# A convolution, spectral and feed-forward hybrid on one core: the first normalisation on GpSimd, a new order of work, two images per loop body

## The reference, cut to what matters

```python
# layer 0
h = depthwise_conv_7x7(x) + conv_b
h = (h - mean_c(h)) * rsqrt(var_c(h) + 1e-5) * ln_g + ln_b        # the "first normalisation"
h = gelu(h @ w1 + b1) @ w2 + b2
x = h * layer_scale + x
# layer 1, on tokens t = x as (image, 3136, 96)
u = relu(bn1(ln(t) @ aw1))                                        # second normalisation
X = fft over the 3136 tokens of u
y = ifft(relu(complex scale and shift of X)).real
t = t + bn2(y @ aw2)
t = t + quantised_linear2(relu(quantised_linear1(ln(t))))         # third normalisation
```

## Time and profile before

| | |
|---|---|
| runs shown | 4677.69 us median of 3 (4676.67 to 4680.09) |
| the profiled execution | 4678.17 us; its span 4676.4 us, so 1.8 us lie around the span |
| busy in the span | PE 3989.9 us (85%), DVE 3461.5 (74%), ACT 2285.2 (49%), POOL 1390.6 (30%) |
| chain that ended last | PE 36%, DVE 30%, time without a named wait ("issue") 12%, ACT 2%, POOL 2%, DMA 1% |
| first in the chain by line | PE 993 (M2) 9%, PE 987 (M1) 7%, PE 1026 (B) 5%, DVE 892 (B) 5%, DVE 831 writing `h_norm` 4%, DVE 831 writing `xn2` 4% |
| TensorE's clock, mean | 0.966 of full |
| DMA | 532.48 MB at a mean of 114 GB/s |

### The profile page before, as it was taken

The page is one execution under the profiler, slowest core; times in us unless marked ns, Lnnn a source line. Parts: engine busy times, 40 slices in busy tenths (PEclk is TensorE's granted clock), DMA queues, the critical chain, the costliest instruction groups (busy, mean ns, idle before and its releaser), DMA issues.

```text
span 4676.4 us, 88192 instructions
## 1 busy us (share of the span) xinstructions
PE 3989.9 (85%) x22802; PEld 2808.8 (60%) x22802; DVE 3461.5 (74%) x11833; ACT 2285.2 (49%) x4610; POOL 1390.6 (30%) x1572
## 2 busy tenths in 40 slices
PE   5999969888888888888888888888888888888885
PEld 3444436666666666666666666666666666666664
DVE  2333346788888888888888888888888888888876
ACT  2444424455555555555555555555555555555543
POOL 1111233333332333333333333333333232333331
PEclk8999979999999999999999999999999999999986
DMA  6666524344444444444443333343444444444331
GB/s 172 166 169 172 163 71 107 94 111 115 111 113 113 111 112 115 109 113 115 110 114 105 98 102 107 102 108 105 108 113 114 111 113 114 112 112 113 100 91 49
DMA packets 420416, 532.48 MB, mean 114 GB/s; under 512 B 220047, under 2 KB 378493, under 8 KB 404413
## 3 DMA queue, kind: packets, MB, share of 16 engines
q1 hardware_dynamic: 405920, 510.40, 40.6%
q10 hardware_dynamic: 14272, 20.04, 1.7%
HBM read 295.18 MB, written 235.12 MB: 113 GB/s over the span
## 4 chain that ended last, share of the span: by engine, by line
PE 36%; DVE 30%; issue 12%; ACT 2%; POOL 2%; DVEq 1%; DMA 1%; ACTq 0%; POOLq 0%; SPq 0%
PE psum L993 9%; PE psum L987 7%; PE psum L1026 5%; DVE minus L892 5%; DVE xn L831 4%; DVE h_norm L831 4%; DVE plus L892 4%; DVE stats L809 3%; PE psum L1035 2%; PE psum L1007 2%; DVE act L875 2%; PE psum L1015 2%; PE psum L1049 2%; DVE h L922 1%; PE psum L1062 1%
## 5 line engine op out<-in xcount | busy, mean ns | idle before, releaser
L683 POOL TENSOR_TENSOR scales<-sums,minus_half 112x4 f32<-112x4 f32 (+1 forms) x480 | 636.6, 1355 | 2191.8 <-DVE sums L824 2191.8
L712 POOL TENSOR_TENSOR both<-plus,minus 96x224 f32<-96x224 f32 (+1 forms) x1024 | 618.2, 623 | 587.3 <-DVE minus L892 502.9
L993 PE MATMUL psum<-hid,w_sb 128*96 128x448 f32 x1344 | 592.8, 580 | 6.5 <-ACT hid L748 2.0
L987 PE MATMUL psum<-hn,w_sb 96*128 96x448 f32 x1344 | 557.2, 547 | 8.4 <-ACT h L796 6.9
L767 ACT ACTIVATE uw<-psum,spec 96x224 f32<-96x224 f32 (+1 forms) x1024 | 445.6, 511 | 157.5 <-PE psum L1026 154.9
L386 PE MATMUL c_psum<-c_xt,c_toeplitz 128*112 128x448 f32 x1152 | 476.6, 551 | 50.3 <-ACT c_xt L328 26.9
L414 DVE TENSOR_SCALAR c_h<-c_psum,c_bias 112x448 f32<-112x448 f32 x192 | 199.0, 1036 | 413.1 <-PE c_psum L386 413.1
L892 DVE SCALAR_TENSOR_TENSOR plus<-psum,spec,uw 96x224 f32<-96x224 f32 (+1 forms) x1024 | 426.8, 417 | 63.5 <-ACT uw L767 63.0
L748 ACT ACTIVATE hid<-psum,b_sb 128x448 f32<-128x448 f32 x672 | 419.7, 635 | 104.1 <-PE psum L987 61.9
L892 DVE SCALAR_TENSOR_TENSOR minus<-psum,spec,uw 96x224 f32<-96x224 f32 (+1 forms) x1024 | 425.8, 416 | 0.0
L1035 PE MATMUL psum<-aw_sb,both 96*112 96x96 f32 x3712 | 410.3, 263 | 4.7 <-ACT hid L748 4.7
(11 more groups left out here) (85 smaller groups left out, 6549.5 us busy)
## 6 DMA issues: line engine op xcount, KB each, us to landing
outer_spectrum<-outer SPq DMA_DIRECT2D x448, 168.0 KB
inner<-outer_spectrum SPq DMA_DIRECT2D x32, 2016.0 KB
c_xpad<-x SPq DMA_DIRECT2D x96, 392.0 KB, 11.2
h_tokens<-c_h SPq DMA_DIRECT2D x24, 1568.0 KB, 8.4
h<-h_tokens SPq DMA_DIRECT2D x32, 1176.0 KB, 13.3
x_sb<-x SPq DMA_DIRECT2D x32, 1176.0 KB, 7.3
residual_stream<-t SPq DMA_DIRECT2D x224, 168.0 KB, 2.1
inner_inverse<-unmixed SPq DMA_DIRECT2D x224, 168.0 KB, 2.3
```

The costliest lines, as they stand in the source:

```text
L683: nc.gpsimd.tensor_tensor(scales[which][:, at:at + w], su[:, :, 5], minus_half[:, 0:w], ALU.pow).then_inc(ready.sem, 1)
L712: last = nc.gpsimd.tensor_tensor(both[:, c % 2, m, 0:w, k * PT // 2:(k + 1) * PT // 2], half(plus), half(minus), ALU.subtract if k else AL ...
L987: pe.matmul(bank("M1", c, m, CW, 128), w1_sb[:, m * 128:(m + 1) * 128], hn[:, c * CW:(c + 1) * CW], start=True, stop=True).then_inc(m1_mad ...
L993: last = pe.matmul(dst, w2_sb[:, m, :], hid[:, c % 2, m, :], start=(m == 0), stop=(m == KF - 1))
```

## The change

- L0N moves from DVE to POOL: DVE's branch and the helper `normalize` go, POOL gets the same four `tensor_scalar` per chunk, with `add` in place of `subtract`; for the first normalisation `sums[..., 3]` therefore holds minus the mean (factor -0.5).
- `variances` no longer writes `sums[..., 3]` for the second normalisation, where nothing reads it; in the other two that instruction goes ahead of the product.
- `STAGES` and `LATER` get new numbers for every step and engine.
- The first steady turn (n = 2) is written out, and the loop has 14 iterations of two turns.

```diff
 STAGES = {
-    1: {"M1": (-3, 11.8, NC), "M2": (7, 11.8, NC), "T": (13, 11.8, NC), "W1": (22, 11.8, NC), "A": (27, 11.8, NC)},
-    2: {"B": (11, 9.3, ND), "W": (24, 9.3, ND), "IB": (28, 8.8, ND)},
-    3: {"AP": (3, 11.5, NC), "S2": (8, 11.5, NC), "N2": (14, 11.5, NC), "T2": (18, 11.5, NC), "F1": (20.5, 12, NC),
-        "G": (25, 11.5, NC), "F2": (32, 11.5, NC)},
-    "next": {"L0S": (34, 3.4, NC), "L0N": (72, 3.3, NC), "HT": (79, 2.8, NC)},
-    "fetch": {"FETCH": (9, 11.5, NC - 3)},
-    "fetch next": {"FETCH NEXT": (78, 1, 3)},
+    1: {"M1": (-0.5, 11.7, NC), "M2": (6.0, 11.8, NC), "T": (12.5, 11.7, NC), "W1": (22.0, 11.9, NC),
+        "A": (25.5, 12.7, NC)},
+    2: {"B": (8.0, 8.7, ND), "W": (18.0, 9.9, ND), "IB": (27.5, 8.9, ND)},
+    3: {"AP": (2.0, 11.1, NC), "S2": (6.5, 11.0, NC), "N2": (12.5, 11.4, NC), "T2": (17.5, 10.8, NC),
+        "F1": (21.0, 12.0, NC), "G": (23.5, 11.8, NC), "F2": (31.0, 12.1, NC)},
+    "next": {"L0S": (35.5, 3.9, NC), "L0N": (94.5, 4.0, NC), "HT": (88.5, 3.0, NC)},
+    "fetch": {"FETCH": (28.5, 10.5, NC - 3)},
+    "fetch next": {"FETCH NEXT": (103.0, 1.4, 3)},
 }
 LATER = {
-    "act": {"W": -0.5, "G": -0.5},
-    "dve": {"B": 3, "M2": 2, "T": 2, "W1": 1, "F2": 2, "AP": 1, "S2": 1, "L0N": -1, "W": -2},
-    "pool": {"B": 4, "T": 3, "S2": 2, "F1": 1},
-    "sp": {"M2": 3},
+    "act": {"F2": 0.5, "T2": -1.0, "B": -0.5, "IB": -0.5, "HT": 0.5, "A": 0.5},
+    "dve": {"B": 1.0, "M2": 0.5, "T": 2.5, "F2": 9.0, "S2": 1.5, "L0N": 0.5, "G": -0.5, "N2": -0.5, "L0S": -10.0},
+    "pool": {"B": 6.5, "T": 5.0, "S2": 5.0, "L0N": -21.0, "L0S": -7.5},
+    "sp": {"M2": -2.0, "IB": -0.5, "A": 12.0, "FETCH": -8.0, "FETCH NEXT": 10.5},
     "pe": {},
 }
...
-            with eng.Fori(2, NB - 1) as n:
-                turn("steady", n)
+            turn("steady", 2)
+            with eng.Fori(0, (NB - 4) // 2) as pair:
+                turn("steady", pair * 2 + 3)
+                turn("steady", pair * 2 + 4)
...
+                    if name == "L0N":
+                        if c == 0:
+                            pool.wait_ge(ln0_ready.sem, ln0_ready.at(n + 1))
+                        b, j = before(n + 1, c, NC, 4)
+                        pool.wait_ge(ht_made.sem, ht_made.at(b, j))
+                        pool.sem_inc(passed, 1)
+                        for j in range(CH):
+                            q = CH * c + j
+                            last = nc.gpsimd.tensor_scalar(
+                                h_norm[:, c % 4, j, :].rearrange("p (k c) -> p k c", c=CC), h[:, :, q, :],
+                                sums[0][:, q, 3:4], scales[0][:, q:q + 1], ALU.add, ALU.mult)
+                        last.then_inc(h_normed.sem, 1)
...
+                if which != 1:
+                    nc.vector.tensor_scalar(su[:, :, 3], su[:, :, 0], 0.5 if which else -0.5, None, ALU.mult)
                 nc.vector.scalar_tensor_tensor(out=su[:, :, 4], in0=su[:, :, 2], scalar=C / 4.0, in1=su[:, :, 2],
-                                               op0=ALU.mult, op1=ALU.mult)
-                nc.vector.tensor_scalar(su[:, :, 3], su[:, :, 0], 0.5, None, ALU.mult).then_inc(step.sem, 1)
+                                               op0=ALU.mult, op1=ALU.mult).then_inc(step.sem, 1)
...
-                    if name == "L0N":
-                        if c == 0:
-                            dve.wait_ge(ln0_ready.sem, ln0_ready.at(n + 1))
-                        b, j = before(n + 1, c, NC, 4)
-                        dve.wait_ge(ht_made.sem, ht_made.at(b, j))
-                        normalize(0, 0, h_norm[:, c % 4, :, :].rearrange("p q (k c) -> p q k c", c=CC),
-                                  h[:, :, part, :].rearrange("p k q c -> p q k c"), CH * c).then_inc(h_normed.sem, 1)
```

More of the change, by code:

```diff
@@ L825, in variances @@
                                                op0=ALU.add, op1=ALU.add).then_inc(seen.sem, 1)
[L827 to L834, removed]
             def turn(kind, n):
@@ L916, in turn @@
                         dve.wait_ge(xt2_made.sem, xt2_made.at(*before(n, c, NC, 2)))
-                        normalize(2, c, xn2[:, c % 2, :, :], t2_rows[:, c % 2, :, :], 0).then_inc(xn2_done.sem, 1)
+                        for j in range(CH):
+                            at = CH * (c % 2) + j
+                            last = nc.vector.tensor_scalar(xn2[:, c % 2, j, :], t2_rows[:, c % 2, j, :], sums[2][:, j, 3:4],
+                                                           scales[2][:, at:at + 1], ALU.subtract, ALU.mult)
+                        last.then_inc(xn2_done.sem, 1)
                     if name == "G":
```

## The result

The changed kernel takes **4620.35 us** (median of 4 runs, 4611.43 to 4629.68), the kernel before, run beside it, 4678.77: a ratio of 0.9876, with a 95% interval of 0.9854 to 0.9897. It is faster by 1.2%. The prediction said 4400 us with a range of 4240 to 4570: right in the sign, wrong in the size, and outside the range. Its profiled execution took 4616.74 us, its span 4614.9.

A forecast was written before the change was run, and what follows sets the result against it. No engine alone bounds the kernel: TensorE and VectorE wait for each other in order. TensorE busy 105.4 plus waits 8.0 gives a turn of 113.4 us, 9.6 less, times 29 is 278: 4678 - 278 = 4400 us, range 4240 to 4570.

The forecast's parts named there:

- the jump: Loop jump over two turns: at most 2.41 us for each of 14 jumps, taken as 0.6, +8 us in all.
- (f): TensorE at B 1 waits for `inner`, whose DRAM round trip from A 6 has less cover: 3.5 us a turn, bounds 0 and 6.
- (a) to (c): TensorE's waits at T2 for N2 and at T for W1's bank go: some 4.2 of 4.27 us at T2 0, most of 3.2 at T.
- (e): TensorE at M1 0 waits for ScalarE's copy for HT 6, now that nothing stands between: 1.0 us a turn.
- (g): TensorE's W1 3 waits for its bank, emptied by VectorE's late M2 4: 2.0 us a turn, bounds 0 and 4.27.
- (h): TensorE's waits at A 6 and F2 6 at the turn's end keep their cause: 1.5 us a turn.
- The sum of waits: TensorE's waits left per steady turn in the new order: 8.0 us.
- (d): VectorE sheds 7.1 us (first normalisation) and 0.6 (unused mean) a turn, so the small waits for it go.
- the normalisation: First normalisation on GpSimd: 300 ns an instruction, 8.4 us a turn (7.5 to 18.7), cost 0 for the last three steps.
- held ports: GpSimd's new instructions slow VectorE beside them: left at 0 a turn, bounds 0 and 6.0 us.
- Slower: GpSimd paces the turn's end: Rival: slow GpSimd instructions delay HT 6; gain used up from 1.1 us each, 4817 us at 1.5; chance 0.12.
- Less: Rival: waits only move and ports are held, so only VectorE's work counts: 4.1 us a turn, 4560 us; chance 0.20.

The follow-up runs named there:

- e1: The changed kernel with one turn per loop body instead of two: 4494.95 us, ratio 0.9607 to the kernel before.
- e4: The kernel before with nothing changed but two turns per loop body: 4865.68 us, ratio 1.0396.
- e2: The changed kernel with SyncE's stores of A and the fetches of the next turn 6 places earlier: 4551.19 us, ratio 0.9722.
- e3: The changed kernel with both one turn per loop body and SyncE's earlier stores of A and next fetches: 4443.75 us, ratio 0.9496.
- e8: e3 with GpSimd's fifth step of the first normalisation ahead of its power for T 6: 4442.56 us, ratio 0.9495.
- e6: e3 with the first normalisation back on VectorE: 4442.42 us, ratio 0.9493 to the kernel before.
- e11: e3 with the unused mean of the second normalisation written again: 4442.74 us, ratio 0.9494.
- e14: e3 with GpSimd subtracting the mean instead of adding minus the mean: 4553.97 us, ratio 0.9732.
- e7: The kernel before, order kept, with only the first normalisation moved to GpSimd, subtracting the mean: 4970.42 us, ratio 1.0610.
- e9: e8 with B a place later on every engine: 4623.64 us, ratio 0.9871 to the kernel before.
- e12: e9 with SyncE's three fetches for the next turn ahead of A 5's store: 4508.25 us, ratio 0.9628.
- e13: e7 with GpSimd adding minus the mean instead of subtracting the mean: 4759.35 us, ratio 1.0177.

## Why the prediction was right or wrong

**The failed step is the jump.** "Bounds 0 and 2.41 per jump ... I take 0.6, +8 us in all": measured per iteration it was 9.0, 125 us (e1), and 13.3 in the old order (e4), both beyond the upper bound. The bound came from VectorE's idle at its own jump, another engine with another body; the row that only one queue fetched in the steady turns was read rightly as a warning, and then priced by a row that cannot show the new case. The Trainium skill's sentence gave the right event, and the prediction gave it a size from that same row. Nor did any term hold the clock: behind each of the 13 waits M1 0 takes 4.5 to 4.9 us for 2.52.

**The second failed step is a sentence of (f)**: "ScalarE's A 5 may wait for A 3's, and what it waits comes off (f), since the edge then begins later". A 5 does wait for A 3's store, and TensorE for A 5 3.4 us at HT 1, but nothing came off: B 1 still waited 57.4 / 16 = 3.6 us for `inner` in the turns that have no jump, which is (f)'s 3.5. The two add up because the wait stands ahead of A 6, and (f) is counted from A 6 on. The queue was named and its price left at nothing; e2 put it at 69 us, and with one turn per iteration (e1 to e3) it is 51.

These two are 176 us of the 220 (e3). **The third is the clock at M1 0.** In e3 TensorE's busy time is 1.9 us a turn over the 105.4 predicted, and M1 0 alone is 2.15 us longer than M1 1 at the edge shown. The sum took off what a slow M2 1 had cost at the old wait and put nothing in for the matmuls behind the new waits at HT.

**What held.** (a) to (c): T2's and T's waits went, 236.0 to 10.2 and 94.1 to none. (e): M1 0 waits 0.8 to 1.0 us for the last HT copy, as predicted. (f): 3.6 against 3.5 in the turns that have the wait (2.1 in e3), and `inner` proved to be the end that the turn hangs on (e8). (g): 42.3 us, 1.5 a turn against 2.0, but mostly at W1 1 and not at W1 3. (h): nothing was left of the 1.5; A 6 and F2 6 wait no more.

**What was right by luck.** The sum of waits: e3 has 7.7 us a turn where 8.0 stood, but 2.1 of them are at HT for GpSimd, which stood at 0, and (f) and (h) came out smaller by 2.9. Also (d) and the normalisation. VectorE's 7.1 us and the mean were counted as part of the gain; e6, e8 and e11 show that in the new order they are worth nothing in sum, and the gain is the order's alone. One instruction cost 0.41 us alone and 0.54 in the mean, not 0.30. In this profile's groups of GpSimd in the steady turns:

```profile
L703 POOL TENSOR_SCALAR h_norm<-h,sums,scales 112x96 f32<-112x96 f32 x812 | 425.6, 536 | 104.5 <-PE psum L984 104.4
```

That is 15 us a turn against 8.4, and "Cost 0" for the last three steps became 0.9 a turn at HT, 2.1 in e3.

The Trainium skill, "SBUF — State Buffer", "Who interferes with whom", has GpSimd and a two-port VectorE instruction exclude each other. The trace agrees: a step of four took 1.62 us at 2767.7, with VectorE idle, and 3.45 at 2772.1, beside F2's and G's instructions. The prediction left held ports at 0 for VectorE's side: N2's instruction took 453 ns in the mean where it took 353, but also 408 in e6, so only a part of that is the normalisation's, and TensorE's waits for N2 are 10.2 us in all.

**The rivals.** "Slower: GpSimd paces the turn's end" did not happen, but it was near: it is what e14 does to e3, at 0.84 us an instruction in the mean, and what e7 does to the kernel before. The sign of the mean, which is part of the change and which the prediction did not price, is what kept it away. "Less" gave 4560 for the reverse of the truth: it had VectorE's work count and the order not. The range ended at 4570, just above this rival; with a jump bounded at 2.41 us, 34 us in all, nothing in the sum asked for more.

**A version that beats both** is e3, 4443.75 us, 5.0% under the kernel before; e6, with no normalisation on GpSimd at all, is as fast.

## What to carry to other kernels

Price a longer loop body by the instructions of its largest engine and not by the turn that it saves: here a doubled body cost TensorE a fetch and a slow spell at every jump, 125 of the 185 us that the rest of the change gave (e1). When a step is moved in an in-order DMA queue, ask of each transfer behind it who waits for it and what it waits for: A 3's store cost 69 us here (e2), and fetching `t_old` sooner gave back 115 of the 181 us that e9 had lost (e12). After a gain, look for the end that the period hangs on (here A 6 to B 1): work taken off another engine was then worth nothing (e8, e11). And give the clock a term: waits of 3.2 us in all ahead of M1 0 took another 2 us with them (e3).

## What the runs showed of the hardware

- A GpSimd `tensor_scalar` of 112x96 with the mean and the scale from a column took 0.69 us with subtract and multiply and 0.42 with add and multiply (medians, e7 and e14 against e13).
- A jump that makes TensorE fetch its instructions again cost 5 to 11 us of idle time (13 of them in the changed kernel), and the six matmuls behind it took 4.5 to 4.9 us in place of 2.52.
- SyncE was held 4.2 to 6.4 us (median 4.7) by the issue of the third and smallest load of `inner`, 42 KB, as before; what e9 adds is its price, since the fetches of `t_old` stood behind it in SyncE's order.
